# Moving the step tables of a fused feed-forward and attention kernel, and starting its scores 12 steps ahead instead of 15

## The reference

```python
x = x + 0.5 * ffn(layernorm(x), weight, bias, delta_w, delta_act)
x = x + attn(layernorm(x), wq_w, wq_b, wk_w, wk_b, wv_w, wv_b)
x = x + 0.5 * ffn(layernorm(x), weight, bias, delta_w, delta_act)

# attn: per head of 8, with rotary position coding of q and k
scores = jnp.einsum('bhqd,bhkd->bhqk', q, k) / np.sqrt(HD)
out = jnp.einsum('bhqk,bhkd->bhqd', softmax(scores), v)

# ffn: both operands rounded per block of 32, scale from the block's largest magnitude
x_q = mxfp4_pseudo_quant(x, delta_act)
w_q = mxfp4_pseudo_quant(weight, delta_w.reshape(-1, 1))
return jnp.einsum('bsd,od->bso', x_q, w_q) + bias
```

## Time and profile before

| | |
|---|---|
| runs | 617.38 us median of 3 (612.36 to 617.54) |
| profiled execution | 620.8 us, span 618.9 us |
| granted clock of PE, mean | 0.944 |
| PE, DVE, ACT, POOL busy | 517.9, 452.4, 393.2, 250.7 us |
| row maxima L908 | 512 of 681 ns |
| exponentials L639 | 512 of 606 ns |
| DMA moved | 30.84 MB |

### The profile page before, as it was taken

How to read it: one execution, slowest core, us unless ns; L and a number is a source line. 1 busy time by engine, 2 the same in 40 slices (tenths; PEclk the granted TensorE clock), 3 DMA queues, 4 the chain that set the end, 5 groups by cost and what they waited for, 6 DMA issues and landing times.

```text
span 618.9 us, 10478 instructions
## 1 busy us (share of the span) xinstructions
PE 517.9 (84%) x2724; PEld 177.0 (29%) x2724; DVE 452.4 (73%) x1037; ACT 393.2 (64%) x773; POOL 250.7 (41%) x452
## 2 busy tenths in 40 slices
PE   0453999799979998999889897999889995999862
PEld 0121233233323332333223232333323331322211
DVE  6674879587988797768957598869957784788214
ACT  8343149386958684678837585768747683667750
POOL 6010266215753665345723465346723543011300
PEclk9999999799999998899979899999969996999995
DMA  5016102600161015100350015100440026000000
GB/s 159 1 34 143 27 3 53 153 2 1 35 146 27 20 36 128 45 19 11 92 107 19 6 35 131 44 18 19 96 96 19 2 59 147 13 9 1 6 14 17
DMA packets 21685, 30.84 MB, mean 50 GB/s; under 512 B 4333, under 2 KB 19321, under 8 KB 19321
## 3 DMA queue, kind: packets, MB, share of 16 engines
q1 hardware_dynamic: 21624, 30.13, 20.3%
HBM read 21.34 MB, written 8.39 MB: 48 GB/s over the span
## 4 chain that ended last, share of the span: by engine, by line
PE 54%; DMA 11%; DVE 9%; POOL 8%; issue 7%; ACT 6%; SPq 4%; POOLq 0%; ACTq 0%; DVEq 0%
PE sc L1120 15%; PE ot L1133 14%; PE st L1109 12%; DMA feat_k<-parts_k 8%; PE misc L1074 4%; DMA parts_k<-qkparts_k 3%; SPq L333 3%; DVE negmax L908 2%; ACT probs L639 2%; PE misc L1055 2%; PE misc L1098 2%; POOL rstd_f L404 2%; SPq L335 1%; PE misc L1073 1%; POOL qkparts_k L496 1%
## 5 line engine op out<-in xcount | busy, mean ns | idle before, releaser
L908 DVE TENSOR_REDUCE negmax<-sc 128x1 f32<-128x512 f32 x512 | 331.9, 681 | 106.6 <-PE sc L1120 106.2
L639 ACT ACTIVATE probs<-st 128x512 f32<-128x512 f32 x512 | 273.4, 606 | 127.1 <-PE st L1109 126.4
L1120 PE MATMUL sc<-feat_k,feat_q 96*128 96x512 bf16 x512 | 197.8, 411 | 38.6 <-DMA feat_k<-parts_k 23.9
L1109 PE MATMUL st<-feat_q,feat_k 99*128 99x512 bf16 x512 | 162.1, 395 | 2.9 <-ACT probs L639 2.2
L1133 PE MATMUL ot<-probs,vfeat 128*32 128x512 f32 x1024 | 143.2, 634 | 1.0 <-ACT probs L639 1.0
L1120 PEld LDWEIGHTS sc<-feat_k,feat_q 96*128 96x128 bf16 x512 | 51.2, 100 | 208.7 <-DVE negmax L908 127.4
L1109 PEld LDWEIGHTS st<-feat_q,feat_k 99*128 99x128 bf16 x512 | 50.7, 100 | 71.2 <-ACT probs L639 38.8
L467 POOL TENSOR_TENSOR cosd<-qkv,rope 128x256 f32<-128x256 f32 x28 | 20.4, 728 | 57.6 <-ACT qkv L602 57.5
L404 POOL TENSOR_TENSOR rstd_pj<-ve_pj,nhalf 128x4 f32<-128x4 f32 x8 | 8.3, 1038 | 75.2 <-DVE nm_pj L779 75.2
L446 POOL TENSOR_SCALAR maxparts<-negmax 128x16 bf16<-128x16 f32 x32 | 8.3, 258 | 67.9 <-DVE negmax L908 67.9
L1040 PE MATMUL misc<-identb,xq_f 128*128 128x128 bf16 x64 | 6.9, 236 | 28.9 <-DVE xq_f L842 28.3
(11 more groups left out here) (143 smaller groups left out, 529.0 us busy)
## 6 DMA issues: line engine op xcount, KB each, us to landing
feat_q<-parts_q SPq DMA_DIRECT2D x48, 192.0 KB
feat_k<-parts_k SPq DMA_DIRECT2D x48, 192.0 KB
parts_q<-qkparts_q SPq DMA_DIRECT2D x24, 128.0 KB, 2.3
parts_k<-qkparts_k SPq DMA_DIRECT2D x24, 128.0 KB, 2.3
xres<-in_L_attn_x_dram SPq DMA_DIRECT2D x8, 256.0 KB, 5.1
out_dram<-xres SPq DMA_DIRECT2D x8, 256.0 KB, 2.3
feat_q<-maxrows SPq DMA_DIRECT2D x32, 12.0 KB
wload<-in_L_ffn_weight_dram SPq DMA_DIRECT2D x1, 64.0 KB, 2.4
```

Of the source, the lines that this page charges most:

```text
L639: nc.scalar.activation(probs[:, s % US, j * S:(j + 1) * S], st[:, bank(2 * s + j), :], ACT.Exp, scale=SCALE).then_inc(exp_done, 1)
L908: nc.vector.tensor_reduce(negmax[:, g, j:j + 1], sc[:, bank(16 * g + j), :], AX.X, ALU.max, negate=True).then_inc(sc_maxed, 1)
L1109: nc.tensor.matmul(st[:, bank(2 * s + j), :], feat["k"][par][0:MROWS, h, kb * P:(kb + 1) * P], feat["q"][par][0:MROWS, h, :], start=True, ...
L1120: nc.tensor.matmul(sc[:, bank(16 * g + j), :], feat["q"][par][0:SROWS, h, t * P:(t + 1) * P], feat["k"][par][0:SROWS, h, :], start=True, s ...
```

## The change

Scores run 12 steps ahead instead of 15, so they begin at step 20 of the slot before and a unit's scores end at step 3 of a unit; the max rows' stages move three steps later with them. The first feed-forward stands three steps earlier (its turn and product one). The projection starts three steps earlier, its four products stand at 25, 26, 27 and 30, the turns of q and k four steps earlier, and all that follows (rest, mid, low, write, load) too. The values' steps (`putv`) stay. The second feed-forward's turn and product stand one step later.

```diff
-LEAD = 15
+LEAD = 12
-FFN1 = dict(stats=3, rstd=4, norm=6, amax=8, scale=10, expo=11, quant=11, turn=15, mul=16)
-PROJ = dict(stats=20, rstd=21, norm=23, turn=25, qkv=(27, 30, 31, 35), rope=(28, 31, 34, 35), turnqk=(38, 39),
-            rest=(39, 39), mid=(41, 41), low=(42, 42), write=41, load=44, putv=(31, 31, 35, 37))
-FFN2 = dict(stats=7, rstd=9, norm=11, amax=13, scale=16, expo=16, quant=19, turn=22, mul=23, store=29)
-MAX = dict(split=1, turn=2, copy=2, load=2)
+FFN1 = dict(stats=0, rstd=1, norm=3, amax=5, scale=7, expo=8, quant=8, turn=14, mul=15)
+PROJ = dict(stats=17, rstd=18, norm=20, turn=22, qkv=(25, 26, 27, 30), rope=(26, 28, 30, 31), turnqk=(34, 35),
+            rest=(35, 35), mid=(37, 37), low=(38, 38), write=37, load=40, putv=(31, 31, 35, 37))
+FFN2 = dict(stats=7, rstd=9, norm=11, amax=13, scale=16, expo=16, quant=19, turn=23, mul=24, store=29)
+MAX = dict(split=4, turn=5, copy=5, load=5)
```

## The result

The changed kernel takes 666.45 us (median of 4 runs, 662.53 to 670.46) where the kernel before takes 617.46 (612.36 to 617.68): ratio 1.0815, 95% interval 1.073 to 1.09. That is slower, as forecast, and by more than forecast: 635 was predicted, 650 was the upper end of the range. The profiled execution is the fastest of the four, 662.53 us, its span 660.7.

A forecast was written before the change was run, and what follows sets the result against it. A loop through k's low part, feature loads and max rows bounds each batch: period 66.8 + 2.1 + 1.0 = 69.9 us. Start 115.1, six periods 419.4, tail 101.8 and 1.9 around the span give 638.2, scaled to 635; range 611 to 650.

The forecast's parts named there:

- What is late next: At `st` of step 16: the wait moves from features to max rows, which land behind the twelve feature loads; chance 0.71.
- The rival that the rows do not hold `st` up: At step 16: rows pass, or loads end earlier, so no wait is left in a slot; 579 us, chance 0.13.
- Start: Before the periods: first exponential at 81.1 us instead of 84.58, first resumption at 115.1 instead of 118.18.
- tail: From the last resumption to the end: 101.8 us instead of 99.8, with step 16 and three more steps with scores.
- low leg: Slot's first exponential to end of k's low part: 16.9 us instead of 23.2, -6.3 with queueing on ACT.
- The rival without it (13.8): No queueing on ACT: low part ends at 13.8 us, -0.9 a period, 607 us; with the no-change case together 0.16.
- DMA leg: End of low part to resumption: 12.9 as before, 0.6 for SP's bunched writes, 6.7 for loads and rows.
- From resumption to the next slot: From `st` of step 16 to slot's end: step 16 adds 1.0, the fourth projection 1.1, together +2.1 us a period.
- The clock's part: After each long wait at step 16 PE's clock drops to 1.2 GHz, costing +1.0 us a period on the mean.
- The edit at nothing: POOL: FFN1's `quant` ahead of FFN2's `rstd` delays ACT's norm some 2.5 us, hidden at step 16; otherwise 1 to 2 a batch.
- Wait at step 16: PE's `st` waits for the max rows seven times, 4 to 8 us each, 20 us after `qkparts_k` ends.
- Between 3.1 and 2.1: Period terms summed to +3.1 us, -0.9 with nothing queued; +2.1 was taken, as PE's catching up was uncertain.

The follow-up runs named there:

- Experiment 6: Kernel before with PROJ `load` 44 -> 41 only, so SP issues the twelve feature loads ahead of unit 2's max rows: 694.6 us, 1.1205.
- experiment 1: Changed kernel with the feature loads at step 14 instead of 8, behind the max rows of unit 2 in SP's queue: 645.56 us, 1.0414.
- experiment 7: Changed kernel with ACT issuing each unit's max rows itself, behind its own copy of them, instead of SP: 670.88 us, 1.0821.
- Experiment 3: Changed kernel with FFN2's `quant` on POOL at step 20 instead of 19, behind `split_max`: 658.16 us, 1.0576.
- Experiment 8: Changed kernel with all three edits, FFN2's turn and product back at 22 and 23: 634.48 us; then also the kernel before's PROJ table with `load=46`: 626.86 us.
- experiment 2: Changed kernel with FFN1's `quant` on POOL at step 9 instead of 8, behind FFN2's `rstd`: 673.7 us, 1.0863.
- all three edits: Changed kernel with the edits of experiment 1, experiment 2 and Experiment 3 together: 619.51 us, 0.9996 of before.

## Why the prediction was right on the wait and short in its size

**What is late next: right.** The seven waits of `st` for the max rows are there, 21 us after the low part of k ends (20 predicted), and in each slot the rows land within 0.7 us of the last feature (259.75 for 259.09 in the slot shown). Experiment 6 shows it alone, 1 takes it away. The Trainium skill, "DMA: Bandwidth & Descriptors", section "Queues, rings and completion order", has each DMA engine consume one ring in order, and experiment 6 agrees: 18.9 to 20.5 us from the low part to `st` with its rows, where the features took 18.7 in the slot of before that was read. "The max rows cannot land before the features do" says more than the rule. The same section calls completion not first in, first out, and in two of after's seven slots the rows land 0.1 and 0.4 us ahead of the last feature load; so they do in before behind the issue of 185.47 (189.56 for 190.14). The same section has an engine take turns between queue rows, packet by packet; by that the rows of experiment 7 would have passed, and the runs show that they did not. The rival that the rows do not hold `st` up is out. What was said for it rests on a misreading: the 26 small packets of the earlier trace rows are all of 4 bytes, and such packets go with the feature loads, twelve to a load; the 48 of the rows, of 256 bytes, all move from 187.91 on.

**Start, tail and the low leg: right.** First exponential 80.26 (81.1 predicted), first resumption 113.62 (115.1), tail 660.7 - 558.64 = 102.1 (101.8). From the slot's first exponential to the end of the low part 16.3 us on the mean of six slots (16.9), for 23.2 before: the queueing on ACT, worked out from its order, is there. The rival without it (13.8) is out.

**DMA leg: short by 0.8.** From the end of the low part to resumption it takes 21.0; 20.2 was forecast (12.9 as before, 0.6 for SP's bunch, 6.7 for the loads). All six writes of parts stand behind the max rows of step 5, and SP issues them in one bunch:

```profile
236.22 0.75 SPq L302 DMA_DIRECT2D feat_q<-maxrows  x1
237.25 0.58 SPq L319 DMA_DIRECT2D parts_q<-qkparts_q  x1
...
240.52 0.61 SPq L319 DMA_DIRECT2D parts_k<-qkparts_k  x1
242.87 0.82 SPq L333 DMA_DIRECT2D feat_q<-parts_q  x1
```

The low part of k ended at 239.16; the parts land 3.7 later for 2.3 in the earlier trace rows. The bunch was foreseen, but costs 1.4 in this slot and not 0.6: that is the 0.8.

**From resumption to the next slot: the step that failed.** Step 16 and the fourth projection, "+2.1", and "+1.0" of clock were forecast; +6.2 is measured (36.9 us for 30.7), 3.1 more. The clock's part did not come: over these six stretches the granted clock is 0.95 on the mean, and 0.93 before; behind the short wait at 259.88 it stayed at 1.00. "1.2 GHz each time" was wrong, so some 4 us have to be found in the work and its waits. The sum named the work that enters this stretch and took the rest of it as unchanged. But the table moves the max rows' stages by three steps and leaves FFN2's `quant` at 19, and on POOL's queue `split_max` now comes at 20, right behind 3.6 us of `quant`, with PE's turn one step later. "The turns of FFN2 move by one step, nothing waits" looked at the turns alone. Experiment 3 gives its price: 1.5 us in step 21, 1.7 a period over steps 16 to 31, and 2.4 points of the ratio, with intervals of 1 point either way. The rest, some 2 us, stands in steps 22 to 26, where FFN2's product now meets the consecutive projections: steps 24 to 26 take 3.62, 2.05 and 3.34 us for 1.88, 1.44 and 2.01. Experiment 8 shows that it cannot simply be moved back, since `quant` then is too late; what part of it is PE's and what ACT's was not told apart.

**The edit at nothing: right.** FFN1's `quant` ahead of `rstd` delays ACT by 2.60 us, was said to be hidden by the wait at step 16, and experiment 2 shows that it is: without it the wait for the rows doubles and the time does not fall. Its price once the cover is gone, "1 to 2 a batch", may have been low: step 11 gives back 2.7 us a slot (4.47 to 1.74), and steps 0 to 15 take 3.7 us less with all three edits than with edit 1 alone, while edit 3 alone leaves them at 37.6. Edits 1 and 3 without 2 were not run, so the share of edit 2 in that is argued, not shown.

**Wait at step 16: too long.** 4 to 8 us each were predicted and 0.2 to 2.1 are there in the middle slots. Steps 0 to 15 take 37.6 us and not 29.6, so `st` comes later by itself: the sum held nothing for this second path beside the loop. The loop over the rows still sets the period, but in the middle slots by 1.5 us only (experiment 1).

**Between 3.1 and 2.1.** The terms summed to +3.1 a period and the prediction took +2.1, by a guess on how PE would catch up. It did not. With all terms as measured (+6.2 - 6.9 + 8.1 = +7.4) the result is six times 7.4 less 4.6 at the start and 2.3 more in the tail: 42 us, which is the difference of the spans, 660.7 - 618.9. The range allowed +5.7 upwards, since it doubled terms that were on the list and held nothing for one that was not.

## What to carry to other kernels

A small transfer that an engine waits for is best *issued* ahead of bulk ones; behind them it landed with the last of them here, and a queue of its own did not change that. For a step that is moved, write down for every in-order queue it stands in what is right ahead of it and right behind it, the small stages that stay in place included: more than a third of the unforeseen loss (1.5 to 1.7 of 4.3 us a period) was one large POOL stage ahead of a small one. Where two late paths run side by side, take them away together before judging either: moving FFN1's `quant` gained nothing alone, and with the loads out of the way the first half of a slot fell from 36.2 to 32.5 us.

## What the runs showed of the hardware beyond that

A DMA issued on ACT's queue moved no packet for 3.8 to 6.6 us while SP's loads were under way, against 1.4 us with the DMA engines quiet; what the two queues share was not found. A load of 24 rows of 8 KB moves as 24 such packets and twelve of 4 bytes, with twelve packets under way at a time: that alone keeps the DMA share near 0.75. And one step number (`load` from 44 to 41) cost 12%, 694.6 us for 619.87, with PE's granted clock down from 0.944 to 0.867 in the profiled executions.
